# Another order of work at the beginning of a cross-attention and ternary feed-forward kernel

## The reference

```python
q = (layernorm(x) @ Wq.T)                     # 16 heads of 32
k, v = split(ctx @ Wkv.T)
attn = softmax(where(pad_mask[:, None, :, None], q * scale @ k.T, -1e9))
x = x + tanh(g_xattn) * (attn @ v)
x = x + tanh(g_ffn) * bitffn(layernorm(x))    # 512 -> 2048 -> 512, ternary weights, 8-bit activations
```

## Time and profile before

| | us |
|---|---|
| median of 3 runs | 2000.84 (1998.82 to 2001.43) |
| profiled execution | 2002.04 |
| its span | 2000.3 |
| mean granted TensorE clock | 0.988 |
| busy: PE, DVE, ACT, POOL | 1886.8, 1252.8, 1069.3, 623.3 |

### The profile page before, as it was taken

One profiled execution on the slowest core, in us unless ns is written; L12 is line 12 of the kernel. 1 busy time (PEld: TensorE's weight loads), 2 busy tenths in 40 slices (PEclk: granted clock), 3 DMA queues, 4 the chain that ended last, 5 costly groups with the idle time before them and its releaser, 6 DMA issues. The chain is left out here.

```text
span 2000.3 us, 39426 instructions
## 1 busy us (share of the span) xinstructions
PE 1886.8 (94%) x13866; PEld 1468.3 (73%) x13923; DVE 1252.8 (63%) x2285; ACT 1069.3 (53%) x1695; POOL 623.3 (31%) x644
## 2 busy tenths in 40 slices
PE   4999999999999999999999999999948999999997
PEld 3888888888888888888888888888834444444443
DVE  3555555554545454555555555555549999999996
ACT  3444444444444443444344444444327999999997
POOL 2101011110101020110101011210018999999994
PEclk9999999999999999999999999999978999999999
DMA  3011211111112111111112111111032222222221
GB/s 116 27 48 59 74 48 43 47 43 47 45 56 80 43 47 43 49 43 47 43 50 72 59 47 43 47 43 43 21 112 76 91 94 94 94 84 89 94 73 38
DMA packets 56104, 120.61 MB, mean 60 GB/s; under 512 B 5597, under 2 KB 5597, under 8 KB 55934
## 3 DMA queue, kind: packets, MB, share of 16 engines
q1 hardware_dynamic: 56062, 120.07, 18.5%
HBM read 101.64 MB, written 29.43 MB: 66 GB/s over the span
## 5 line engine op out<-in xcount | busy, mean ns | idle before, releaser
L412 ACT ACTIVATE prob<-psum,nmax 114x750 f32<-114x750 f32 x256 | 225.4, 885 | 251.5 <-DVE nmax L600 251.5
L338 POOL TENSOR_TENSOR y_l<-y,y_h 128x750 fp32r<-128x750 f32 x96 | 161.8, 1706 | 553.7 <-ACT y_h L398 553.1
L605 DVE TENSOR_TENSOR k_l<-psum,k_h 128x376 fp32r<-128x376 f32 (+1 forms) x256 | 139.7, 546 | 281.3 <-ACT k_h L403 280.9
L403 ACT ACTIVATE k_h<-psum 128x376 fp32r<-128x376 f32 (+1 forms) x256 | 124.0, 484 | 356.0 <-PE psum L839 354.4
L600 DVE TENSOR_REDUCE nmax<-psum 114x1 f32<-114x750 f32 x256 | 228.4, 934 | 103.3 <-PE psum L828 99.1
L839 PE MATMUL psum<-y_h,wkv_h 128*128 128x376 f32 (+1 forms) x768 | 277.2, 361 | 1.1 <-DVE q_l L593 1.1
L839 PE MATMUL psum<-y_h,wkv_l 128*128 128x376 f32 (+1 forms) x768 | 256.1, 333 | 0.0
L839 PE MATMUL psum<-y_l,wkv_h 128*128 128x376 f32 (+1 forms) x768 | 255.9, 333 | 0.0
L849 PE MATMUL psum<-wkv_h,y_h 128*125 128x512 f32 x576 | 237.4, 412 | 0.0
L849 PE MATMUL psum<-wkv_l,y_h 128*125 128x512 f32 x576 | 228.2, 396 | 0.0
L1432 PE MATMUL psum<-w_q,hq_t 128*128 128x512 bf16 x895 | 204.7, 382 | 24.6 <-ACT yo L1288 24.5
(11 more groups left out here) (117 smaller groups left out, 3373.4 us busy)
## 6 DMA issues: line engine op xcount, KB each, us to landing
y<-in_ctx_t SPq DMA_DIRECT2D x32, 1125.0 KB, 8.0
w_part<-in_w_t SPq DMA_DIRECT2D x32, 512.0 KB, 8.2
xb<-in_x SPq DMA_DIRECT2D x56, 256.0 KB, 2.7
ab<-attn_rows SPq DMA_DIRECT2D x56, 256.0 KB, 2.9
out_rows<-yo SPq DMA_DIRECT2D x56, 256.0 KB, 2.0
attn_rows<-vmean_rows SPq DMA_DIRECT2D x32, 336.0 KB
xa<-in_x SPq DMA_DIRECT2D x32, 112.0 KB
attn_rows<-attn SPq DMA_DIRECT2D x32, 112.0 KB
```

The costliest lines, as they stand in the source:

```text
L338: pool.tensor_tensor(y_l[:, slot, c, :], y[:, c, :], y_h[:, slot, c, :].bitcast(F32), ALU.subtract).then_inc(a_yl, 1)
L403: act.activation(k_h[:, g, s0:s1], ps_proj[k_bank[par][g, hf]][:, 0:s1 - s0], ACT.Copy).then_inc(a_kh, 1)
L412: act.activation(prob[:, e, :], ps_score[e][0:RP], ACT.Exp, bias=nmax[:, i:i + 1], accum_out=den[:, i:i + 1]).then_inc(p.exp, 1)
L605: dve.tensor_tensor(k_l[:, g, s0:s1], ps_proj[k_bank[par][g, hf]][:, 0:s1 - s0], k_h[:, g, s0:s1].bitcast(F32), ALU.subtract).then_inc(a_k ...
```

## The change

What it does, part by part:

1. The mask is loaded as 32 rows of 224 bytes, one per partition, and reduced there to `live_b` [32, 4]. A transfer from SyncE's queue, behind `wq` and the gates, lays `live_b` out as the one row `live`, and the three small steps to `most` come after the low parts of the weights. `a_flag` counts to 4.
2. The mask, x of batches 0 and 1, and the mask's columns are issued from ScalarE's queue, ahead of its first work; the last four wait for VectorE's fills.
3. The V half of `wkv` is loaded first, each half has a semaphore, and ScalarE and VectorE take V's half first. TensorE waits for V's low part ahead of the first `v_chunk` and for K's ahead of the first `k_half`, no longer for both ahead of everything.
4. The low part of the first `y` is made by VectorE, between the moments of `xa` and its normalisation; GpSimd begins with the deviation. VectorE makes `wkv_l` behind the normalised `xa`.

```diff
-        mask_bytes = stage[0:1, 0:B * S // 4].bitcast(U8)
-        at = B * S // 4
+        mask_bytes = stage[0:B, 0:S // 4].bitcast(U8)
+        at = S // 4
...
             def _(sp):
                 sp.dma_start(y[:], ctx_t[0].rearrange("(c p) m -> p c m", p=128)).then_inc(a_y, 16)
-                for i in range(2):
-                    sp.dma_start(wkv_raw[:, :, D * i:D * i + D], wkv_in[:, :, D * i:D * i + D]).then_inc(a_wkv, 16)
-                sp.dma_start(mask_bytes, mask_row).then_inc(a_mask, 16)
-                sp.wait_ge(a_zero, 2)
-                sp.dma_start(mcol8[0:R, :], mask_col).then_inc(a_mask, 16)
-                sp.dma_start(mcol8[RM:RM + R, 0:(B - 1) * NBLK], mask_col[:, NBLK:]).then_inc(a_mask, 16)
+                sp.dma_start(wkv_raw[:, :, D:2 * D], wkv_in[:, :, D:2 * D]).then_inc(a_wv, 16)
+                sp.dma_start(wkv_raw[:, :, 0:D], wkv_in[:, :, 0:D]).then_inc(a_wk, 16)
...
-                load_pair(0)
                 sp.dma_start(wq_raw, wq_t.rearrange("(c p) n -> p c n", p=128)).then_inc(a_wq, 16)
                 for i, g in enumerate((g_xattn, g_ffn)):
                     sp.dma_start(gates_in[:, i:i + 1], one_row(g).to_broadcast([128, 1])).then_inc(a_gin, 16)
+                sp.wait_ge(a_flag, 1)
+                sp.dma_start(live[:], live_b[:]).then_inc(a_live, 16)
...
                 pool.wait_ge(a_const, 3)
-                split_y(0, 0)
                 rstd(last, 0)
...
             def _(act):
+                act.dma_start(mask_bytes, mask_row.rearrange("a (b s) -> (a b) s", s=S)).then_inc(a_mrow, 16)
+                act.wait_ge(a_zero, 2)
+                act.dma_start(xa[0:R, :], rows(x_flat, 0, RB)).then_inc(last.x, 16)
+                act.dma_start(xa[RM:RM + R, :], rows(x_flat, 1, RB)).then_inc(last.x, 16)
+                act.dma_start(mcol8[0:R, :], mask_col).then_inc(a_mask, 16)
+                act.dma_start(mcol8[RM:RM + R, 0:(B - 1) * NBLK], mask_col[:, NBLK:]).then_inc(a_mask, 16)
                 act.wait_ge(a_y, 16 + ONE)
                 for c in range(CC):
                     act.activation(y_h[:, 0, c, :], y[:, c, :], ACT.Copy).then_inc(a_yh, 1)
-                for i in range(2):
+                for i, arrived in ((1, a_wv), (0, a_wk)):
                     w = slice(D * i, D * i + D)
-                    act.wait_ge(a_wkv, 32)
+                    act.wait_ge(arrived, 16)
                     act.activation(wkv_h[:, :, w], wkv_raw[:, :, w], ACT.Copy).then_inc(a_whi, 1)
...
             def _(dve):
                 dve.memset(mcol8[:], 0).then_inc(a_zero, 1)
                 dve.memset(xa[:], 0.0).then_inc(a_zero, 1)
-                for i in range(2):
-                    w = slice(D * i, D * i + D)
-                    dve.wait_ge(a_whi, i + 1)
-                    dve.tensor_tensor(wkv_l[:, :, w], wkv_raw[:, :, w], wkv_h[:, :, w].bitcast(F32), ALU.subtract).then_inc(a_wlo, 1)
...
-                dve.wait_ge(a_mask, 48)
-                dve.memset(kind[:], 0).then_inc(a_flag, 1)
-                dve.tensor_reduce(live[:], mask_bytes.rearrange("a (b k r) -> a b k r", k=NBLK, r=R), AX.X, ALU.max).then_inc(a_flag, 1)
-                dve.tensor_copy(mcol[:], mcol8[:]).then_inc(a_mcol, 1)
+                dve.wait_ge(a_mrow, 16)
+                dve.tensor_reduce(live_b[:], mask_bytes.rearrange("b (k r) -> b k r", r=R), AX.X, ALU.max).then_inc(a_flag, 1)
...
                 moments(last, 0, 32 + ONE)
+                dve.wait_ge(a_mask, 32)
+                dve.tensor_copy(mcol[:], mcol8[:]).then_inc(a_mcol, 1)
+                for c in range(CC):
+                    dve.wait_ge(a_yh, c + 1 + ONE)
+                    dve.tensor_tensor(y_l[:, 0, c, :], y[:, c, :], y_h[:, 0, c, :].bitcast(F32), ALU.subtract).then_inc(a_yl, 1)
+                dve.wait_ge(a_mcol, 1)
                 normalise(last, 0, RB)
+                for n, i in enumerate((1, 0)):
+                    w = slice(D * i, D * i + D)
+                    dve.wait_ge(a_whi, n + 1)
+                    dve.tensor_tensor(wkv_l[:, :, w], wkv_raw[:, :, w], wkv_h[:, :, w].bitcast(F32), ALU.subtract).then_inc(a_wlo, 1)
+                dve.wait_ge(a_live, 16)
+                dve.tensor_reduce(live_rest[:], live[:, :, 0:NBLK - 1], AX.X, ALU.max).then_inc(a_flag, 1)
...
             def _(pe):
                 pe.wait_ge(a_const, 3)
-                pe.wait_ge(a_wlo, 2)
...
                         turn(last, t + 1)
                         pe.wait_ge(a_yl, CC * (b + 2) + ONE)
                         pe.wait_ge(a_kl, k0)
+                        pe.wait_ge(a_wlo, 1)
                         v_chunk(1, 0, 0)
+                        pe.wait_ge(a_wlo, 2)
                         pe.wait_ge(last.xe, t + 2 + ONE)
                         k_half(1, 0, 0, 0)
```

More of the change, by code:

```diff
@@ L96, in gated_cross_attention_bit_ffn @@
         gates_in = sb("gates_in", [128, 2])
+        live_b = sb("live_b", [B, NBLK], I32)
         live = sb("live", [1, B, NBLK], I32)
@@ L149, in gated_cross_attention_bit_ffn @@
         a_mask, a_gin, a_y = sem("a_mask"), sem("a_gin"), sem("a_y")
-        a_wq, a_wkv, a_w = sem("a_wq"), sem("a_wkv"), sem("a_w")
+        a_wq, a_wk, a_wv, a_w = sem("a_wq"), sem("a_wk"), sem("a_wv"), sem("a_w")
+        a_mrow, a_live = sem("a_mrow"), sem("a_live")
         a_const, a_zero, a_head = sem("a_const"), sem("a_zero"), sem("a_head")
@@ L190, in __init__ @@
                 eng.reg_mov(self.n, 0)
-                eng.wait_ge(a_flag, 5)
+                eng.wait_ge(a_flag, 4)
                 eng.load(self.most, most[0:1, 0:1])
@@ L653, in _ @@
                 moments(last, 0, 32 + ONE)
-                normalise(last, 0, RB)
+                dve.wait_ge(a_mask, 32)
[4 more added lines that the diff above has]
+                dve.wait_ge(a_mcol, 1)
+                normalise(last, 0, RB)
+                for n, i in enumerate((1, 0)):
[4 more added lines that the diff above has]
+                dve.tensor_reduce(live_rest[:], live[:, :, 0:NBLK - 1], AX.X, ALU.max).then_inc(a_flag, 1)
+                dve.wait_ge(a_flag, 2)
+                dve.scalar_tensor_tensor(out=kind[:], in0=live_rest[:], scalar=2.0, in1=live[:, :, NBLK - 1],
+                                         op0=ALU.mult, op1=ALU.max).then_inc(a_flag, 1)
+                dve.wait_ge(a_flag, 3)
+                dve.tensor_reduce(most[:], kind[:], AX.X, ALU.max).then_inc(a_flag, 1)
                 dve.wait_ge(a_gate, 1)
```

## The result

The changed kernel takes 1987.25 us in the median of 4 runs (1984.78 to 1987.85), the kernel before 2001.13 of 4 beside it: 13.9 us less, ratio 0.9926, 95% interval 0.9911 to 0.9942. In a second set of runs on another occasion it was 1987.30 (6 runs) against 2002.10 (11 runs), 14.8 us less, ratio 0.9928, 0.9915 to 0.9940. The forecast was 1985.8, and the range 1983.5 to 1989.5 holds both medians.

What follows compares the result with a forecast made beforehand. PE's summed work was taken as the bound, so its start shifts everything behind it. First k_half moving from 32.31 to 17.25 gains 15.06 us: 2000.84 - 15.06 = 1985.8 us, range 1983.5 to 1989.5.

Steps and rivals of the forecast that it cites:

- The bound: Attention phase: PE's summed work bounds; all after its first work moves as one piece, first k_half 15.06 us earlier.
- The mask: Start, DVE: the mask's reduction over 32 partitions takes 0.35 us instead of 7.57, taking 7.2 us off the path.
- ACT's queue: Start: issues of 0.46 to 0.5 us and the table load end by 4.7, costing nothing; y's high part starts at 6.65.
- The landing of x: Start: x, issued from ACT's queue and sharing the engines with y, lands at 5.4 to 7.3 us.
- rival (c): Start: x doesn't pass the weights and lands by 11 us; gain 11.0, 1989.8 us; chance 0.07. Sign: x_stats past 7.3.
- The low part of y on DVE: Start: three low parts at 0.86 us each, ending near 10.1; then normalisation, xa at 10.85.
- V's half first: Start: V's half lands at 8.6 to 9.1; v_chunk waits for its low part alone, starting at 12.75 instead of 28.32.
- What is late next: Before first k_half: ACT's copy of wq, then xn_t at 17.0, set k_half at 17.25; DVE's chain has 0.5 us spare.
- The live list: DVE, after the weight parts: waits for a small transfer landing after about 15, then 0.6 us of steps; k_l at 19.6.
- Rival (e): DVE's first k_l: a late live list holds PE, making the kernel slower, 2001 to 2005 us; chance 0.02.
- Rival (d): After 60 us: the start moves but the end doesn't, 2000.8 us; chance 0.04.
- rival (b): PE's start: pauses keep the clock low longer, 1.7 us lost; gain 13.4, 1987.5 us; chance 0.12.

Runs made afterwards that it cites:

- the combined kernel: The changed kernel with x queued behind y on SyncE's queue and the turned x emptied ahead of wq's copy; median of 5 runs 1986.54 us.

## Why the prediction was right, and where it wasn't

**The bound.** That PE's order of work moves as one piece is borne out: k_half 13.93 us earlier, the first batch's rows 13.91.

**The mask.** 0.37 us against 0.35, and alone it moved k_half by 8.05 against 7.8.

**ACT's queue.** The issues took 0.32 to 0.62 us, the table load came behind them (3.69 to 4.97, forecast until 4.7) and cost nothing, y's high part began at 6.43 against 6.65. This held. **The landing of x didn't**: forecast 5.4 to 7.3, measured 8.72. I gave it 2.4 us of fixed time and a share of the engines beside y. x_stats began 6.6 us after the second half of x was issued. This is the step that failed. The sign of my rival (c) appeared (x_stats past 7.3), but not its mechanism: (c) had x behind the weights, by 11, and x landed before V's half (9.8) and K's (12.0), whose issues at 1.26 and 1.80 stood ahead of or among its own. The move to ACT's queue was worth 3.0 us of x's landing (11.73 back on one queue behind the weights), not nothing. The sign was too coarse to tell a late x from one that doesn't pass. Queueing x behind y on one queue got it in at 7.64. Why a transfer of 224 KB on its own queue needs that long beside 1125 KB, the runs don't say; only that the columns aren't the reason.

**The low part of y on DVE.** 2.63 us for three against 2.6. I allowed for x at 7.3 "moves the end from 10.1 to 11.0"; with x at 8.72 the end was 12.37, by the same working. GpSimd's deviation was taken at 1.1 us and needed 2.1, hidden behind the low parts. I had used the rule of the Trainium skill ("GPSIMD Engine Reference", "Specifications", that GpSimd and VectorE contend for their SBUF interfaces when VectorE has two SBUF inputs) for DVE's side only; the trace agrees on GpSimd's side too, and far more strongly, 0.19 alone against 0.89 beside DVE. On DVE's side it can be as strong: the copy of the mask's columns, which has one SBUF input and so isn't the case of that rule as I used it, took 0.23 us, and 1.85 beside GpSimd's low parts of y.

**V's half first.** It landed at 9.8, not by 9.1, off the chain here since DVE came to it at 12.94. Undone it costs 2.0 us.

**What is late next.** This conclusion was wrong. xn_t ended at 17.14 as forecast (17.0), but DVE's chain, to which I gave 0.5 us to spare, was later than it: v_chunk ended at 18.38. The loss against the forecast is 18.38 - 17.25 = 1.13 us, and most of it comes from x's landing (0.74 us of it came back with x behind y): xa ended 2.2 us late (13.03 against 10.85), v_chunk began 2.1 late (14.84 against 12.75), of which the 0.5 of spare time took one part and v_chunk's own length another, 3.54 us instead of 3.99, the clock rising under it: 2.09 - 0.51 - 0.45 = 1.13.

**The live list.** DVE's steps on it began at 16.28, without a wait, and k_l at 20.70 against ACT. Rival (e) had no part. Rival (d) neither.

**The clock.** Named as rival (b) at a price of 1.7 us with 0.12. It went the other way in this execution, helped by 0.45 us, which was luck, and cost the combined kernel about 1 us. It belonged into the range on both sides of every case, not into a case of its own.

**The number.** 2000.84 - 13.93 would have been 1986.9; measured 1987.25 and 1987.30. The forecast of 1985.8 is 1.4 to 1.5 too low, by the 1.13 of the start and the noise of the medians. Range and sign were right for the reason given, except for the engine that sets the start: the miss in x's landing was bigger than the miss in the number, since 0.5 us of spare time and 0.45 us of the clock's luck took part of it.

## What to carry to other kernels

At the start of a kernel with one full engine, write down the chain up to that engine's first work, and ask for each load when it lands beside the others, not when it is issued: x on a queue of its own landed later than x queued behind the larger y. Let an engine that must wait for a load do first what is already there. And a last step is only "last" if its rivals are more than the uncertainty of a landing away; here 0.5 us of spare time was less than the 1.4 us by which a landing was missed.

## What the runs showed of the hardware

The start of PE's upper clock level comes at no fixed place in its work: in kernels with the same order of work on PE it came 2.9 to 5.9 us after v_chunk's first matmul, which moves the whole kernel by about 1 us (the first batch's rows at 89.74 instead of 88.89). Matmuls of constants ahead of it made the first v_chunk run at 0.40 us a matmul instead of 0.63. A thin stretch of PE of 3.3 us in 5 is followed by a fall of the clock in some executions and not in others, 0.9 to 1.6 us each. A small step on GpSimd took 0.19 us alone and 0.89 beside VectorE's subtraction of two tiles; a small copy on VectorE took 0.23 us, and 1.85 beside GpSimd's. 224 KB of x on a queue of its own landed at 8.4 to 8.7 us, queued behind 1125 KB of y on one queue at 7.5 to 7.6.
